# Attention scores in 64-query blocks: array parts of 64 by 64, 640 instead of 768 score columns a reduction, late masks partly on TensorE

## What is computed

```python
x = x + 0.5 * ffn(layernorm(x))       # 128 -> 512 -> 512 -> 512 -> 128: silu gate, two exact gelus
x = x + linear_attention(layernorm(x))  # no softmax
x = x + 0.5 * ffn(layernorm(x))       # the same weights again
x = x + 0.5 * moe(layernorm(x))       # top 2 of 8 experts, chosen by the block's first token
x = x + attention(layernorm(x))       # the layer that the change is about
x = x + 0.5 * moe(layernorm(x))
```

```python
q, k, v = heads(W_Q x), heads(W_K x), heads(W_V x)     # 16 heads of 8
q, k = rope(q), rope(k)
scores = einsum('bhqd,bhkd->bhqk', q, k) * scale       # 256 by 256 for each head
scores = where(causal, scores, -inf)
out = softmax(scores) @ v;  out = W_O out
```

## Time and profile before

| | us |
|---|---|
| median of 3 runs (lowest, highest) | 651.84 (649.85, 653.08) |
| the profiled execution | 652.16 |
| its span from the first to the last instruction | 650.4 |
| TensorE's granted clock, mean over the span | 0.994 of full speed |

### The profile page before, as it was taken

How to read it: one execution, slowest core, us unless ns; L and a number is a source line. 1 busy time by engine, 2 the same in 40 slices (tenths; PEclk the granted TensorE clock), 3 DMA queues, 4 the chain that set the end, 5 groups by cost and what they waited for, 6 DMA issues and landing times.

```text
span 650.4 us, 14027 instructions
## 1 busy us (share of the span) xinstructions
PE 615.8 (95%) x5210; PEld 466.2 (72%) x5210; DVE 487.3 (75%) x1262; ACT 485.6 (75%) x816; POOL 306.1 (47%) x476
## 2 busy tenths in 40 slices
PE   4899999999999999999999999988999999999997
PEld 3677878888887887888778887765555666656665
DVE  6767566675675777675978768799988989888846
ACT  5799778787887687787788777724777857877892
POOL 1402202321311525222638354576888766767683
PEclk9899999999999999999999999999999999999999
DMA  9300000000000002100002035454444323122002
GB/s 290 109 1 1 1 0 2 1 2 1 1 1 2 0 2 58 40 1 1 1 26 72 2 90 154 155 165 144 122 122 139 113 81 112 55 90 89 10 3 68
DMA packets 41886, 37.80 MB, mean 58 GB/s; under 512 B 2940, under 2 KB 37020, under 8 KB 41816
## 3 DMA queue, kind: packets, MB, share of 16 engines
q1 hardware_dynamic: 41816, 36.87, 18.4%
HBM read 21.92 MB, written 14.68 MB: 56 GB/s over the span
## 4 chain that ended last, share of the span: by engine, by line
PE 66%; DVE 14%; ACT 9%; issue 5%; DMA 2%; POOL 2%; SPq 1%; DVEq 0%; ACTq 0%; POOLq 0%
PE PSA L1000 20%; PE PSA L1004 20%; PE PSA L1227 6%; DVE MX L1414 3%; PE PSA L1019 3%; DVE G L1292 3%; PE PSA L1213 3%; PE PSA L1179 2%; ACT PSA L1461 2%; PE PSA L1156 2%; DMA QS<-MT 2%; ACT G L1457 1%; PE PSA L1163 1%; PE PSA L1186 1%; PE PSA L1197 1%
## 5 line engine op out<-in xcount | busy, mean ns | idle before, releaser
L1000 PE MATMUL PSA<-ah,WH 128*128 128x512 f32 x320 | 130.3, 407 | 0.5 <-DVE G L1292 0.5
L1414 DVE TENSOR_REDUCE MX<-PSA 128x6 f32<-128x768 f32 x128 | 117.9, 949 | 13.8 <-PE PSA L1186 13.1
L1461 ACT ACTIVATE PSA<-PSA,SC 128x512 f32<-128x512 f32 x128 | 84.7, 662 | 55.0 <-PE PSA L1004 54.4
L1004 PE MATMUL PSA<-al,WH 128*128 128x512 f32 x320 | 125.4, 392 | 0.0
L1553 ACT ACTIVATE PB<-PSA 128x768 f32<-128x768 f32 x128 | 98.6, 813 | 28.9 <-PE PSA L1213 27.6
L1000 PE MATMUL PSA<-bh,WH 128*128 128x512 f32 x256 | 104.8, 410 | 2.7 <-DVE G L1292 2.3
L1583 POOL TENSOR_SCALAR VE<-MV 128x4 f32<-128x4 f32 x46 | 11.4, 247 | 194.4 <-DVE MV L1267 194.4
L1004 PE MATMUL PSA<-bl,WH 128*128 128x512 f32 x256 | 100.3, 392 | 0.0
L1643 POOL TENSOR_SCALAR_AFFINE_SELECT PB<-PB 128x512 f32<-128x512 f32 x128 | 80.2, 636 | 36.0 <-ACT PB L1553 34.0
L1297 DVE TENSOR_TENSOR al<-PSA,ah 128x512 fp32r<-128x512 f32 x64 | 44.0, 687 | 52.7 <-ACT ah L1468 52.2
L1000 PEld LDWEIGHTS PSA<-ah,WH 128*128 128x128 f32 x320 | 60.5, 189 | 13.3 <-issue 0.7
(11 more groups left out here) (163 smaller groups left out, 1282.7 us busy)
## 6 DMA issues: line engine op xcount, KB each, us to landing
KS<-dk SPq DMA_DIRECT2D x32, 192.0 KB
QS<-dq SPq DMA_DIRECT2D x32, 192.0 KB
dk<-CB SPq DMA_DIRECT2D x16, 192.0 KB, 2.3
dq<-CB SPq DMA_DIRECT2D x16, 192.0 KB, 2.5
VA<-in_ones SPq DMA_DIRECT2D x5, 512.0 KB, 4.7
X<-in_x SPq DMA_DIRECT2D x8, 256.0 KB, 6.8
dk<-CB SPq DMA_DIRECT2D x16, 128.0 KB, 2.0
dq<-CB SPq DMA_DIRECT2D x16, 128.0 KB, 1.9
```

Source lines behind the costliest of these rows:

```text
L1000: e.matmul(o, WH[:, col:col + 128], hi, start=first, stop=False)
L1004: return e.matmul(o, WH[:, col:col + 128], low, start=False, stop=last)
L1414: e.tensor_reduce(MX[:, u % 2, 1:4, :].rearrange("p t (l g) -> p l t g", l=2)[:, :, :, g], PSA[:, b:b + 2, 0:384].rearrange("p l (t k) -> ...
L1461: e.activation(bank(b), bank(b), ACT.Gelu, scale=SC[:, k:k + 1]).then_inc(a_gelu, 1)
```

## The change

First passes: the 256 queries are cut in four blocks of 64. Partitions 0 to 63 hold queries 0 to 63 (64 keys, columns 0 to 63) and queries 192 to 255 (256 keys, columns 64 to 319), partitions 64 to 127 hold queries 64 to 127 (128 keys) and 128 to 191 (192 keys). So 320 columns a head are reduced, 640 a pair. Each matmul takes 64 rows and 64 columns of the array: 4 for the mask, 8 for the scores. The partial maxima are in segments of 64 keys, the joining reduction (`peak`) is two instructions on 64 partitions each, and `max_out` puts the queries back in order by a matmul with a permuted identity (ISB). Second passes: keys in blocks of 64, 8 matmuls for 4. In some of them (`kind` "m", chosen in the plan when POOL's planned time is over 2 us behind TensorE's) 4 more matmuls add the mask, and POOL's affine_select falls away: in the built order 40 of the 128. `opening` writes the constant rows for a lot of blocks with 4 DMAs (`rows`; lots of 3 and 2 blocks) and `ones` after the block's `reloc`. First passes of blocks 0 to 2 have priority 1.5 (`FIRST`). `SHIFT` has other numbers, and keys for more kinds of jobs.

```diff
-QUEUED = 1.0
+QUEUED = (2.0, 1.0)
+FIRST = (3, 1.5)
+BEHIND = 2.0
...
 SHIFT = {
-    ("attend", 0): -0.23, ("attend", 1): 0.32, ("attend", 2): -0.07, ("attend", 3): 0.31, ("attend", 11): -0.03,
...
+    ("after", 0, 3): 0.14, ("after", 0, 4): 0.13, ("after", 1, 1): -0.35, ("after", 1, 4): -0.12,
...
-            self.add(2.5, self.attend(2 * c + h, a, va), of=("attend", 2 * c + h))
+            self.add(1, self.attend(2 * c + h, a, va), of=("attend", 2 * c + h))
...
-        for n in range(KEPT):
-            m = 1 if n < 3 else 2
+        for m, lot in ((1, LOTS[0]), (2, LOTS[1])):
...
-            self.qfree[n] = [self.dead[m - 1]]
-            self.vfree[n] = [self.put("ones", i=n, x=m, src=self.dead[m - 1])]
+            self.put("rows", i=m - 1, x=m, src=self.dead[m - 1])
+            for n in lot:
+                self.qfree[n] = [self.dead[m - 1]]
+            while self.turn["reloc"] <= lot[-1]:
+                yield
+            for n in lot:
+                self.vfree[n] = [self.put("ones", i=n, x=m, src=self.dead[m - 1])]
...
-        self.add(self.lead, self.peaks(u, rl), "h", ("peaks", u))
+        self.add(FIRST[1] if u < FIRST[0] else self.lead, self.peaks(u, rl), "h", ("peaks", u))
...
+            m = "m" if self.clock["G"] > self.clock["P"] + BEHIND else ""
...
                 elif st.name == "pass1":
-                    for k in range(2):
-
+                    for x in range(2):
                         for h in range(2):
-                            e.matmul(PSA[:, b + h, 0:384].rearrange("p (t k) -> p t k", t=3)[:, 0::2, 64 * k:64 * k + 64],
-                                     IM[64 * h:64 * h + 64, k, :], MK[64 * h:64 * h + 64, k, :, 64 * k:64 * k + 64],
-                                     start=(k == 0), stop=False, skip_group_check=True)
-                    for h in range(2):
-                        e.matmul(PSA[:, b + h, 0:128], Q[64 * h:64 * h + 50, g, 0:128], K[64 * h:64 * h + 50, g, 0:128],
-                                 start=False, stop=False, skip_group_check=True)
-                    for h in range(2):
-                        t = e.matmul(PSA[:, b + h, 128:384], Q[64 * h:64 * h + 50, g, 128:256],
-                                     K[64 * h:64 * h + 50, g, :], start=False, stop=True, skip_group_check=True)
+                            o = PSA[64 * x:64 * x + 64, b + h, 64 * x:512 - 64 * x].rearrange("p (t k) -> p t k", t=2)
+                            e.matmul(o[:, :, 0:64], IM[64 * h:64 * h + 64, 0, 0:64], MK[64 * h:64 * h + 64, 0, :, 0:64],
+                                     start=True, stop=False, skip_group_check=True)
+
+                    for q, at in (((0, 1), (0, 0)), ((3, 2), (64, 128))):
+                        for x in range(2):
+                            for h in range(2):
+                                n = 64 * q[x] + 64
+                                t = e.matmul(PSA[64 * x:64 * x + 64, b + h, at[x]:at[x] + n], Q[64 * h:64 * h + 48, g, n - 64:n],
+                                             K[64 * h:64 * h + 48, g, 0:n], start=False, stop=True, skip_group_check=True)
...
                 elif st.name == "pass2":
+                    m = st.kind == "m"
                     for k in range(2):
+                        for x in range(2):
+                            for h in range(2):
+                                o = PSA[64 * x:64 * x + 64, b + h, 0:384].rearrange("p (t q) -> p t q", t=3)
+                                t = e.matmul(o[:, 1, :] if k else o[:, 0::2, :],
+                                             K[64 * h:64 * h + 52, g, 128 * k + 64 * x:128 * k + 64 * x + 64],
+                                             Q[64 * h:64 * h + 52, g, 128 * k:256], start=(k == 0), stop=not m,
+                                             skip_group_check=True)
+                    for x in range(2 * m):
+
                         for h in range(2):
-                            o = PSA[:, b + h, 0:384].rearrange("p (t q) -> p t q", t=3)
-                            t = e.matmul(o[:, 1, :] if k else o[:, 0::2, :],
-                                         K[64 * h:64 * h + 52, g, 128 * k:128 * k + 128],
-                                         Q[64 * h:64 * h + 52, g, 128 * k:256], start=(k == 0), stop=True,
-                                         skip_group_check=True)
+                            o = PSA[64 * x:64 * x + 64, b + h, 0:256].rearrange("p (t q) -> p t q", t=2)
+                            t = e.matmul(o[:, :, 64 * x:64 * x + 64], MK[64 * h:64 * h + 64, x, 0, 64 * x:64 * x + 64],
+                                         IM[64 * h:64 * h + 64, x, 64 * x:64 * x + 64].rearrange(
+                                             "p (o q) -> p o q", o=1).to_broadcast([64, 2, 64]),
+                                         start=False, stop=True, skip_group_check=True)
...
-                    e.tensor_reduce(MX[:, u % 2, 1:4, :].rearrange("p t (l g) -> p l t g", l=2)[:, :, :, g],
-                                    PSA[:, b:b + 2, 0:384].rearrange("p l (t k) -> p l t k", t=3), AX,
+                    e.tensor_reduce(MX[:, u % 2, 3:8, :].rearrange("p t (l g) -> p l t g", l=2)[:, :, :, g],
+                                    PSA[:, b:b + 2, 0:320].rearrange("p l (t k) -> p l t k", t=5), AX,
...
-                    e.tensor_reduce(PK[:, u % 2, :, :], MX[:, u % 2, :, :].rearrange("p (q k) h -> p q h k", k=2), AX,
-                                    ALU.max).then_inc(v_peak, 1)
+                    for x in range(2):
+                        R = slice(64 * x, 64 * x + 64)
+                        t = e.tensor_reduce(PK[R, u % 2, :, :], MX[R, u % 2, x:8 + x, :].rearrange(
+                            "p (q k) h -> p q h k", k=4), AX, ALU.max)
+                    t.then_inc(v_peak, 1)
...
-                elif st.name == "pass2":
+                elif st.name == "pass2" and st.kind != "m":
                     P = PB[:, n % SLOTS, 0:2, :, :].rearrange("p t l q -> p (t l) q")
                     w.wait_ge(a_prob, n + 1)
                     e.affine_select(out=P, in_=P, compare_op=ALU.is_ge, fill=0.0, base=0,
```

More of the change, by code:

```diff
@@ L101 @@
 KEPT = 5
+LOTS = (range(3), range(3, KEPT))
 SLOTS = 8
-QUEUED = 1.0
+QUEUED = (2.0, 1.0)
+FIRST = (3, 1.5)
 LEAD = 20
+BEHIND = 2.0
 LONE = 4.0
@@ L218, in put @@
             late = "up_first"
+        if name == "pass2" and st.kind == "m":
+            late = "pass2m"
         for i, (eng, us, *way) in enumerate(TAKES[late]):
@@ L297, in pair @@
             for b in (4, 2, 0):
-                if self.clock[eng] < self.clock["P"] + QUEUED and self.bank[b] is not None and self.bank[b + 1] is not None and self.left(self.bank[b] + self.bank[b + 1]) <= self.clock["P"] + AHEAD:
+                if self.clock[eng] < self.clock["P"] + QUEUED[len(self.dead) > 1] and self.bank[b] is not None and self.bank[b + 1] is not None and self.left(self.bank[b] + self.bank[b + 1]) <= self.clock["P"] + AHEAD:
                     return b
@@ L447, in ending @@
         self.yr.free[0] = [bk]
-        self.add(2, self.first_moe(c, bk) if p else self.attn0(c, bk))
+        self.add(2, self.first_moe(c, bk) if p else self.attn0(c, bk), of=("after", p, c))
     def normed_T(self, kind, c, src):
@@ L836, in build @@
         QS, KS, VA = {}, {}, {}
-        for n in range(KEPT):
-            QS[n] = sb(f"QS{n}", [128, 8, S], BF16)
-            KS[n] = sb(f"KS{n}", [128, 8, S], BF16)
-            VA[n] = sb(f"VA{n}", [128, 2, NH, 32])
+        KQ = [None, None]
+        for k, lot in enumerate(LOTS):
+            KQ[k] = sb(f"KQ{k}", [128, len(lot), 2, 8, S], BF16)
+            for i, n in enumerate(lot):
+                KS[n], QS[n] = KQ[k][:, i, 0, :, :], KQ[k][:, i, 1, :, :]
+                VA[n] = sb(f"VA{n}", [128, 2, NH, 32])
         PB = sb("PB", [128, SLOTS, 3, 2, 128])
@@ L855, in build @@
         s_one = [sem(f"s_one{u}") for u in range(KEPT)]
-        s_far = [sem(f"s_far{u}") for u in range(KEPT)]
+        s_far = [sem(f"s_far{k}") for k in range(2)]
         s_qs = [sem(f"s_qs{u}") for u in range(KEPT)]
@@ L914, in build @@
                 nth_down[id(st)] = k
+        chosen, k = [], 0
+        for st in order.steps:
+            if st.name == "pass2":
+                k += st.kind != "m"
+                chosen.append(k)
         x_age, ages, nth_x, k = {}, {}, {}, 0
@@ L1200, in tensor @@
                     emptied(w, st.emptied)
[L1201 removed]
                     for k in range(2):
[L1203 to L1204 removed]
+                        t = e.matmul(PSA[0:32, b, 128 * k:128 * k + 128], HM[:, k, :, :].rearrange("p m h -> p (m h)"),
+                                     ISB[:, :, :].rearrange("p t q -> p (t q)") if k else IDB[:, :], start=True, stop=True)
                     t.then_inc(p_max, 1)
@@ L1602, in gpsimd @@
                     e.tensor_copy(IDB[:, :], IDN[:, :])
+                    for h in range(2):
+                        e.tensor_copy(ISB[:, h, :], IDN[:, 64 - 64 * h:128 - 64 * h])
```

59 lines of the change are left out of this document (33 added, 26 removed), and 7 rows, old and new, of the table TAKES.

## The result

The changed kernel takes 662.07 us (median, 659.73 to 663.78) against 651.02 for the kernel before: 1.0154 times as long, interval 1.0127 to 1.0181. The forecast was 644 and faster; it is slower, and above the range. The profiled execution took 663.78 us, its span is 662.0.

A forecast was written before the change was run, and what follows sets the result against it. The prediction took VectorE and TensorE, nearly equally full, to bound the long stretch, and VectorE and one SP queue the short one before it. + 1.5 - 7 - 3 + 1 = - 7.5 us gave 644, range 635 to 657.

The forecast's parts named there:

- End of the FFN part, + 1.5: Up to the last FFN matmul: four more first passes and small TensorE terms add 1.5 us (0 to 2.5).
- Until the first second pass, - 7: Last FFN matmul to first second pass: less VectorE work and SP free earlier save 7 us (4 to 9.5).
- rival C: The head start to the first second pass is lost again: 652 us, no change; chance 0.14.
- C's second reason: Before the first second pass, SP holds block 0's maxima after all; part of a no-change case at 652 us.
- The long stretch, - 3: First second pass to last first-pass reduction: 163 us for 166, TensorE now fuller than VectorE; ends - 11 and + 3.
- + 8.4: First second pass to last first-pass reduction: 64 by 64 passes and late masks add 8.4 us to TensorE.
- The middle value: TensorE's passes taken midway between bounds: first pass 0.30 us, second 0.21, second with late masks 0.31.
- Rival D: TensorE pays for weight loads one after another, a first pass 0.38 us: 663 us; chance 0.16.
- Nearly equally full: First second pass to last first-pass reduction: VectorE 89.7% busy and TensorE an estimated 88%, so both limit it.
- B: VectorE was the only limit, first passes cost TensorE 0.23 us, attention stretch 11 us shorter: 636 us; chance 0.13.
- The end, + 1: After the last first-pass reduction: 19 second passes for 20, but dearer on TensorE, add 1 us (0 to 2).
- POOL, nothing: 40 of 128 affine_selects leave POOL, 25 us of its work, counted as no gain by itself.

The follow-up runs named there:

- The two reversals: VA DMAs put ahead of constant rows and reloc in the changed kernel, 649.26 us; VA DMAs moved behind their lot's relocations in the kernel before, 676.86 us.
- the moved copies: Changed kernel, VA transfers still behind the relocations, with ScalarE's copies into VA placed behind its FFN work: 651.2 us, 1.001 of before.
- V: Changed kernel with the DMAs that fill VA issued at the head of each lot, ahead of constant rows and reloc: 649.26 us, 0.9967 of before.
- the two kernels in before's order: Kernel before with 64 by 64 parts in the first passes alone, 653.1 us (1.0029), and in both passes, 649.36 us (0.9985).

## Why the prediction was wrong

*End of the FFN part, + 1.5: measured + 11.4. This step failed.* It priced passes, rotations and keep matmuls, and nothing for moving the VA transfers past twelve relocations on SP's queue, nor named who stands behind their landing. The diff showed it (`ones` put behind the last `reloc`), the 4.7 us to landing stood in the trace. The two reversals and the moved copies show it. In V the stretch is + 0.1, inside the 0 to 2.5 given; whether each of its small terms was right isn't shown.

*Until the first second pass, - 7: measured - 2.0, in V - 5.5.* VectorE did as worked out: joining's start to copy's end is 4.2 us (443.47 to 447.68; 3.8 forecast), the copy is done 12.7 us behind the last FFN subtraction (12.5 forecast), and SP was free to begin, as forecast. The failed part is the 4.6 us from issue to pass, taken over as a constant: behind eight relocations and two VA transfers it was 10.5, of which 3.3 are SP's own issue of the first of the two DMAs. In V's profile, whose maxima were issued at 436.36, it is 7.1. This was rival C's condition (over 21 us: 21.8), and half of C's second reason: SP did not hold the maxima back, but took long to issue them and they landed late. C alone gave 652.

*The long stretch, - 3: measured + 1.7, in V - 0.5 (in a good execution).* Its terms erred on both sides. TensorE: a first pass was to take 0.30 and took 0.20 to 0.22, a second 0.21 and 0.17, the late masks 0.10 and 0.06 to 0.09: by the same counts 111 x - 0.07 + 29 x 0.09 = - 5.2 us (at 0.22, and second passes at 0.17), where + 8.4 stood. The middle value taken there rests on a wrong bound: "L1183's 30 ns" is the mean of 60 ns over a pair, and in the trace of before the two of the pair start 3 ns apart (528.684 and 528.687). What the pass costs is close to the prediction's own 0.187 us of columns in each quadrant. Rival D is dead: in the passes, narrow loads add nothing that the starts show. VectorE: 0.135 an instruction fewer came as said (88.00 us for 111 now, 103.28 for 112 before), but the joining is + 0.51 a block, where + 0.27 stood with + 0.4 as its bound, and the copy + 0.13, which wasn't priced; so 144.8 and not 139 us. The joining's price was taken from the slope of the reductions: that gives 0.275 us for 128 elements, and 0.36 was measured, twice a block. "Nearly equally full" was nearer the truth than B: VectorE's microseconds count by a half and more (2.8 to 5.3 us for 5.8), and so do TensorE's (between the two kernels in before's order, 10.6 us made 8.0 of the profiled stretch and 3.7 of the median). And the clock was missing: 0.97 here. That fillers bring it back is shown; that it fell because the shorter passes leave gaps and 66 fillers are gone is argued. The prediction counted fillers fewer as a gain, "up to - 1.6"; behind the FFNs they hold the clock. With VA first and fillers in, the stretch is 164.1, near the 163 named; that is luck in part, since TensorE was cheaper and VectorE dearer than worked out.

*The end, + 1: + 0.5.* *POOL, nothing: right against the kernel before*, as far as shown: before's order with both passes in 64 by 64 and all 128 masks on GpSimd takes 649.36, V 649.26. Inside the changed order it is not nothing, since GpSimd's idle time, the cover that the prediction named, is planned away there: with the masks back on it this order costs 28 us.

On the Trainium skill's rules weighed there. Twelve matmuls of a first pass take 0.20 to 0.22 us, 17 to 18 ns each in the mean, and the four of a group start 3 ns apart. The Trainium skill (TensorE: Matmul & The Clock Gate, Wait — 56ns, not 53.3ns?) has starts never closer than about 25 ns; across four quadrants this trace disagrees, and by it the first pass would have been the 0.30 I took. The Trainium skill's load time of P / 1.2 (the same page, LDWEIGHTS), an estimated 53 ns for 64 columns, would make 0.64 of twelve loads one by one: measured is a third of it, and the trace has four of these loads starting within 10 ns.

Open: what share of what V's median (649.26) lacks to its fastest execution is clock in each stretch (the clock is one mean for each execution); and why SP's issue of one small DMA takes 3.3 us when large transfers are under way, for which no experiment was made.

## What to carry to other kernels

When a step moves on a DMA queue, write down the bytes now ahead of it, divide by the rate that the trace shows for that window, and name the instruction that waits for its landing and everything behind that on its in-order engine. An engine relieved is not time gained: price each instruction that a split adds or reshapes (here two joinings of 0.36 us for one of 0.21), and look at what new gaps do to the granted clock. Fillers that hold the clock are work, not slack.

## What the hardware showed unexpectedly

- Four quadrants of 64 by 64 in bf16 start their matmuls 3 ns apart; twelve matmuls with 64-column loads take 0.20 to 0.22 us, 17 to 18 ns each. A change between 64 by 64 and 64 by 128 costs 0.10 us each way.
- A reduction over 64 partitions is no cheaper than over 128: 128 elements take 0.36 us either way (two joinings, and the one of the kernels with a single joining). 64 elements took 0.21, so 64 more cost 0.15 here, and 0.07 by the slope of the reductions out of PSUM.
- A transfer of 512 KB lands in 4.7 us ahead of the relocations and in 13.9 to 15.1 behind twelve of them (2.3 MB). With such transfers under way, SP took 3.29 us to issue the first DMA of the maxima, and 0.60 before.
- Two GpSimd fills of 0.53 and 0.31 us do what a transfer of 512 KB did.
